# Queries and keys of an attention kernel: transposed out of the token-wise product instead of projected a second time

## The reference, cut to what matters

```
x = layernorm(tokens)                        # 8 batches, 256 tokens, 128 features
q = split(x @ Wq); k, v = split(x @ Wkv)     # 16 heads, 16 features (q, k), 64 features (v)
q, k, v = q/|q|, k/|k|, v/|v|
attn = relu(q @ k.T) ** 2                    # 256 x 256 per head
out = attn @ v
out = tanh(|out|) * out / |out|
x = tokens + out @ Wout
```

## Time and profile before

| | |
|---|---|
| time, median of 3 runs | 561.87 us (561.01 to 563.82) |
| the profiled execution: its own time, its span | 564.94 us, 563.0 us |
| mean granted clock of TensorE | 0.985 |
| attention | about the first 229 us |
| busy: PE, DVE, ACT, POOL | 530.1, 425.2, 376.3, 327.3 us |

### The profile page before, as it was taken

The page is one execution under the profiler, slowest core; times in us unless marked ns, Lnnn a source line. Parts: engine busy times, 40 slices in busy tenths (PEclk is TensorE's granted clock), DMA queues, the critical chain, the costliest instruction groups (busy, mean ns, idle before and its releaser), DMA issues.

```text
span 563.0 us, 10120 instructions
## 1 busy us (share of the span) xinstructions
PE 530.1 (94%) x3280; PEld 400.5 (71%) x3280; DVE 425.2 (76%) x1006; ACT 376.3 (67%) x676; POOL 327.3 (58%) x276
## 2 busy tenths in 40 slices
PE   5788799999999998899999999999999999999997
PEld 4555467676666665586877787787787888888885
DVE  5966868787879687449849869769769768677675
ACT  6687958677779775364466776776775775755644
POOL 2743929384846564077646756646656656566563
PEclk9899989999999999699999999999999999999999
DMA  8200000000000012910085480650751751761920
GB/s 227 86 16 14 23 15 17 15 15 15 16 16 15 15 24 64 225 30 1 6 199 103 111 197 26 171 137 24 187 123 29 183 122 48 180 139 38 223 62 19
DMA packets 36099, 44.73 MB, mean 79 GB/s; under 512 B 5456, under 2 KB 18896, under 8 KB 36048
## 3 DMA queue, kind: packets, MB, share of 16 engines
q1 hardware_dynamic: 31360, 42.40, 31.7%
q10 hardware_dynamic: 4688, 1.71, 1.3%
HBM read 40.94 MB, written 3.15 MB: 78 GB/s over the span
## 4 chain that ended last, share of the span: by engine, by line
PE 69%; DVE 11%; issue 7%; ACT 7%; POOL 3%; DMA 1%; SPq 0%; ACTq 0%; DVEq 0%; POOLq 0%
PE PS L1220 66%; DVE aT L866 4%; DVE n L845 3%; POOL hl L499 2%; ACT sqv L547 2%; ACT v L540 2%; ACT rl L565 1%; DMA Osb<-wa_dram 1%; PE PS L1355 1%; DMA wbc<-w_dram 1%; PE PS L1341 1%; DVE wfl L911 0%; PE PS L1474 0%; PE PS L1313 0%; ACT n2T L581 0%
## 5 line engine op out<-in xcount | busy, mean ns | idle before, releaser
L499 POOL TENSOR_TENSOR hl<-hb,hh 128x512 fp32r<-128x512 f32 x127 | 164.3, 1294 | 133.7 <-ACT hh L709 129.5
L702 ACT ACTIVATE sil<-PS 128x512 f32<-128x512 f32 (+1 forms) x136 | 80.8, 594 | 82.8 <-PE PS L1220 82.0
L1087 DVE TENSOR_TENSOR PS<-sil,PS 128x512 f32<-128x512 f32 x128 | 88.3, 690 | 61.0 <-PE PS L1220 39.1
L1220 PE MATMUL PS<-fxh,wfh 128*128 128x512 f32 x264 | 105.2, 398 | 3.1 <-issue 1.7
L1220 PE MATMUL PS<-fxl,wfh 128*128 128x512 f32 x264 | 105.0, 398 | 0.0
L1220 PE MATMUL PS<-fxh,wfl 128*128 128x512 f32 x264 | 104.7, 397 | 0.0
L709 ACT ACTIVATE hh<-hb 128x512 fp32r<-128x512 f32 x128 | 80.3, 627 | 32.5 <-DVE hb L1092 30.7
L1092 DVE TENSOR_TENSOR hb<-PS,wbc 128x512 f32<-128x512 f32 x128 | 88.5, 691 | 9.3 <-issue 3.2
L866 DVE SCALAR_TENSOR_TENSOR aT<-PS,rl 128x1024 f32<-128x1024 f32 x64 | 75.2, 1217 | 7.7 <-ACT rl L565 7.6
L565 ACT ACTIVATE rl<-PS 128x1024 f32<-128x1024 f32 x64 | 62.1, 1026 | 21.9 <-PE PS L1220 21.8
L424 POOL TENSOR_TENSOR sr<-n2o,half 128x32 f32<-128x32 f32 x7 | 38.2, 5462 | 51.5 <-DVE n2o L873 51.5
(11 more groups left out here) (175 smaller groups left out, 902.7 us busy)
## 6 DMA issues: line engine op xcount, KB each, us to landing
wbc<-w_dram SPq DMA_DIRECT2D x48, 512.0 KB, 11.6
wbc<-w_dram SPq DMA_DIRECT2D x32, 128.0 KB, 2.9
wbc<-w_dram SPq DMA_DIRECT2D x16, 256.0 KB, 4.2
wfs<-wf_dram SPq DMA_DIRECT2D x32, 98.0 KB, 2.0
band_dram<-zero SPq DMA_DIRECT2D x16, 80.0 KB, 1.7
band<-band_dram ACTq DMA_DIRECT2D x4, 320.0 KB, 3.1
X<-x_dram SPq DMA_DIRECT2D x1, 896.0 KB, 7.7
Osb<-wa_dram SPq DMA_DIRECT2D x3, 256.0 KB, 3.7
```

Of the source, the lines that this page charges most:

```text
L499: g.tensor_tensor(hl[:, n % RING, :], hb[:, n % RING, :], hh[:, n % RING, :].bitcast(F32), ALU.subtract).then_inc(F("hl"), 1)
L702: s.activation(sil[0:rows, n % 2, :], PS[0:rows, G0 + n % 2, :], ACT.Silu).then_inc(F("silu"), 1)
L1087: v_.tensor_tensor(PS[:, bank, :], sil[:, n % 2, :], PS[:, bank, :], ALU.mult).then_inc(F("t"), 1)
L1220: return nc.tensor.matmul(o, w, m, start=start, stop=stop)
```

## The change

The second projection goes. ACT copies the token-wise product of q and k to SBUF, into a buffer `qkt` in which the query heads lie 32 columns apart with zeros between, and PE transposes 128 columns of it at a time into the bank where the padded projection used to go. POOL squares the copy; DVE sums the squares, later in its order than before. A memset on POOL at the start zeroes the query part of `qkt` (576 columns in each of two tiles). The 768 padded weight columns are neither loaded nor split. For the first batch ACT squares the bank itself, after the copies. The diff, cut to its core:

```diff
-FIRST_WEIGHTS = (..., ("in_wp", slice(W_QK, W_V)),
-                 ("in_wq", slice(0, W_QK)))
+FIRST_WEIGHTS = (..., ("in_wp", slice(W_QK, W_V)))
+            qkt = ab("qkt", [P, 2, QT])
 @@ POOL, start
             g.memset(gr[:, :, TOPG:], -9.0).then_inc(cs("sel1"), 1)
+            g.memset(qkt[:, :, 0:NG * QG], 0.0).then_inc(cs("qkz"), 1)
             g.memset(Fpad[:, :, :], 0.0).then_inc(cs("fpad"), 1)
             g.memset(ind[:, :, :], 0.0).then_inc(cs("ind0"), 1)
             inverse_deviation(0)
+            def square_pairs(n, t):
+                pool.wait_ge(A("qkc"), 2 * n + t + 1)
+                pool.wait_ge(A("n2q"), 2 * (n - 1) + t + 1)
+                g.tensor_tensor(by_head(sqqk[:, t, 0:QK]), q_heads(t), q_heads(t), ALU.mult).then_inc(A("sqq"), 1)
+                pool.wait_ge(*freed("qk", n, t))
+                g.tensor_tensor(sqqk[:, t, QK:2 * QK], k_heads(t), k_heads(t), ALU.mult).then_inc(A("sqq"), 1)
 @@ POOL, loop
                     inverse_deviation(b + 2)
+                if b + 1 < B:
+                    square_pairs(b + 1, 0)
+                    square_pairs(b + 1, 1)
                 if b:
                     output_norms(b - 1)
 @@ ACT
-            def square_pairs(n, t):
+            def keep_pairs(n, t):
                 act.wait_ge(*full("qk", n, t))
+                if n:
+                    act.wait_ge(*full("g", n - 1, NQ - 1))
+                    after(act, A("sqq"), 4 * (n - 2) + 2 * t + 2)
+                bank = bank_of("qk", n, t)
+                s.activation(q_heads(t), by_head(PS[:, bank, 0:QK]), ACT.Copy).then_inc(A("qkc"), 1)
+                signal = free_of("qk", n, t) if n else A("qkk0")
+                s.activation(k_heads(t), PS[:, bank, QK:2 * QK], ACT.Copy).then_inc(signal, 1)
+            def first_square_pairs(t):
+                s.activation(sqqk[:, t, :], PS[:, bank_of("qk", 0, t), :], ACT.Square).then_inc(free_of("qk", 0, t), 1)
 @@ ACT, start
-            first_weights_high(3)
...
-            square_pairs(0, 0)
-            square_pairs(0, 1)
+            act.wait_ge(cs("qkz"), 1)
+            for t in range(2):
+                keep_pairs(0, t)
+            for t in range(2):
+                first_square_pairs(t)
             square_values(0, 1)
 @@ ACT, loop
                 relu(NG * b + 1)
                 if more:
-                    square_pairs(n, 0)
-                    square_pairs(n, 1)
+                    keep_pairs(n, 0)
+                    keep_pairs(n, 1)
 @@ DVE, loop
                 squares(NG * b + 1)
-                if more:
-                    pair_norms(n, 0)
-                    pair_norms(n, 1)
...
                 squares(NG * b + 2)
                 if more:
+                    pair_norms(n, 0)
+                    pair_norms(n, 1)
                     value_norms(n, 0)
                     clear_norms(n, 0)
 @@ PE
             def group(n, j):
+                for t in range(2):
+                    if j != 1:
+                        pe.wait_ge(A("qkc"), 2 * n + t + 1)
+                    elif n:
+                        pe.wait_ge(*freed("qk", n, t))
+                    else:
+                        pe.wait_ge(A("qkk0"), t + 1)
                 bank, done = turn("g", n, j)
                 for part in range(2):
-                    cols = slice((2 * j + part) * P, (2 * j + part + 1) * P)
-                    last = split3(PS[:, bank, part * L:(part + 1) * L], wah[:, cols], wal[:, cols],
-                                  xTh[:, :], xTl[:, :])
+                    cols = k_cols(part) if j == 1 else q_cols(j + part)
+                    for t in range(2):
+                        last = nc.tensor.transpose(PS[:, bank, part * L + t * P:part * L + (t + 1) * P], qkt[:, t, cols],
+                                                   ident[:, :])
```

More of the change, by code:

```diff
@@ L40 @@
 NQ = NG // 2 + 1
-WQ_G, WK_G = (0, 1, 4, 5), (2, 3)
-W_QK = 2 * NQ * P
-W_V = W_QK + 2 * QK
+W_QK, W_V = 0, 2 * QK
+QG = P + DK
+QT = NG * QG + 2 * P
 WA = W_V + H * DV
-FIRST_WEIGHTS = (("in_wv0", slice(W_V, W_V + 512)), ("in_wv1", slice(W_V + 512, WA)), ("in_wp", slice(W_QK, W_V)),
-                 ("in_wq", slice(0, W_QK)))
+FIRST_WEIGHTS = (("in_wv0", slice(W_V, W_V + 512)), ("in_wv1", slice(W_V + 512, WA)), ("in_wp", slice(W_QK, W_V)))
 WG0, WU0, WD0, WS0 = 0, NE * P, 2 * NE * P, 3 * NE * P
@@ L204, in hybrid_layer @@
         Z = Sems(ctx, nc, "full0 full5 full6 full7 free0 free5 free6 free7")
-        ld = Sems(ctx, nc, "in_x0 in_x in_wv0 in_wv1 in_wq in_wp in_wo in_wf0 in_wf1 in_sd in_gw in_wb in_bb zeroed")
-        cs = Sems(ctx, nc, "id0 id half rid ind0 ind rm rf sel fpad zero sel1 sdz wah wal wfh wfl sdh sdl")
-        A = Sems(ctx, nc, "stats mv ve rstd xn xTh vraw sqv n2v n2q nm nm_v rr vi vc0 vc vp S relu a av Oc sqO "
+        ld = Sems(ctx, nc, "in_x0 in_x in_wv0 in_wv1 in_wp in_wo in_wf0 in_wf1 in_sd in_gw in_wb in_bb zeroed")
+        cs = Sems(ctx, nc, "id0 id half rid ind0 ind rm rf sel fpad zero sel1 sdz wah wal wfh wfl sdh sdl qkz")
+        A = Sems(ctx, nc, "stats mv ve rstd xn xTh vraw sqv n2v n2q nm nm_v rr vi vc0 vc vp qkc qkk0 sqq S relu a av Oc sqO "
                           "sr sr_half n th nmx rec f1 ff fhi f")
@@ L301, in hybrid_layer, with q_cols, k_cols, q_heads @@
         fxh, fxl, wbc = (fxh0, fxh1), (fxl0, fxl1), (wbc0, wbc1)
+        def q_cols(g):
+            return slice(QG * g - DK * (g % 2), QG * g - DK * (g % 2) + P)
+        def k_cols(f):
+            return slice(NG * QG + f * P, NG * QG + (f + 1) * P)
+        def q_heads(t):
+            slots = qkt[:, t, 0:NG * QG].rearrange("p (g x) -> p g x", x=QG)[:, :, 0:P]
+            return slots.rearrange("p g (r y) -> p g r y", y=SLOT)[:, :, :, 0:DK]
+        def k_heads(t):
+            return qkt[:, t, NG * QG:QT]
+        def by_head(x):
+            return x.rearrange("p (g r d) -> p g r d", g=NG, r=HG)
+        def k_by_group(x):
+            return x.rearrange("p (f r a) -> p f a r", f=2, r=HG)
+        def heads_by_group(x):
+            return x.rearrange("p (f a r) -> p f a r", f=2, a=2)
         block = ctx.enter_context(nc.Block())
@@ L467, in _ @@
             pool.wait_ge(A("vi"), 2)
-            g.tensor_tensor(vc[:, 1, :], vi[:, 1, :], rr[:, 0, 1, H:2 * H], ALU.mult).then_inc(A("vc"), 2)
+            g.tensor_tensor(heads_by_group(vc[:, 1, :]), heads_by_group(vi[:, 1, :]), k_by_group(rr[:, 0, 1, H:2 * H]), ALU.mult).then_inc(A("vc"), 2)
             scale_values(0, 1)
@@ L848, in pair_norms @@
             def pair_norms(n, t):
-                dve.wait_ge(*freed("qk", n, t))
+                if n:
+                    dve.wait_ge(A("sqq"), 4 * (n - 1) + 2 * t + 2)
+                else:
+                    dve.wait_ge(*freed("qk", 0, t))
                 v_.tensor_reduce(n2[:, n % 3, t, 0:2 * H], sqqk[:, t, :].rearrange("p (h d) -> p h d", d=DK),
@@ L1008, in _ @@
             first_weights_low(2)
-            first_weights_low(3)
             value_norms(0, 0)
@@ L1266, in score @@
                 b, g = divmod(i, NG)
-                jq, q0, k0 = WQ_G[g] // 2, WQ_G[g] % 2 * L, g // 2 * L
+                jq, q0, k0 = g // 2 * 2, g % 2 * L, g // 2 * L
                 pe.wait_ge(*freed("g", b, jq))
@@ L1367, in _ @@
             pairs(0, 1)
-            pe.wait_ge(cs("wal"), 4)
             group(0, 0)
@@ L1591, in layout @@
     wk, wv = wkv[:, :, :DK], wkv[:, :, DK:]
[L1592 to L1597, removed]
+    wa = np.concatenate([wq, wk.reshape(D, 2, 2, HG, DK).transpose(0, 1, 3, 2, 4).reshape(D, H * DK), wv.reshape(D, H * DV)], axis=1)
     eg = np.asarray(L0_ffn_expert_gate).transpose(2, 0, 1).reshape(D, E * I)
```

7 lines of the change are left out of this document (3 added, 4 removed).

## The result

| | before | after |
|---|---|---|
| time, median | 562.56 us (561.01 to 563.82, 4 runs) | 572.09 us (570.26 to 575.36, 4 runs) |
| ratio | | 1.019, 95% interval 1.0156 to 1.0223 |
| profiled execution: its time, span, mean clock | 564.94, 563.0 us, 0.985 | 570.26, 568.5 us, 0.979 |
| start of the last squares of the attention | 220.67 us | 228.25 us |

The forecast was 571.6 us. The two medians alone divide to 1.017. The profiled execution is the fastest of the four of the changed kernel, and that of before lies above its median, so the two traces differ by less (5.5 us in span) than the medians (9.5). The last row of the table is the cleaner measure: it leaves out the expert stage, whose length differs between the profiled executions of all kernels here by almost 5 us (337.6 to 342.3), much of it with the clock at its beginning. The attention became 7.6 us longer.

What follows compares the result with a forecast made beforehand. The ACT and DVE exchange was taken to bound the stretch before score(4b+4), PE the rest of each batch. DVE 4.6, start 1.9 and clock 3.2 sum to 9.7 us on 561.87: 571.6 us, range 564.5 to 579.

Steps and rivals of the forecast that it cites:

- What binds: Before score(4b+4), the exchange between ACT and DVE sets the pace, not PE; from that score on PE does.
- DVE: In the loop, pair sums moved ahead of the values' sums add 0.65 us in seven batches: 4.6 us (3.3 to 5.6).
- ACT and POOL in the loop: ACT's four copies and POOL's four products per batch fit into existing waits: 0 us.
- Start: Before score(0), POOL's memset adds 0.86 us and ACT's copies and squares ahead of the kept groups 1.0: 1.9 us together.
- PE: Transposes replacing matmuls save 0.6 us a batch ahead of score(4b+4), where PE waits for DVE: counted as 0.
- Clock: Longer PE waits before score(4b+4) bring two more falls of TensorE's clock: 3.2 us (0 to 10).
- two or more stretches beyond those of before: Sign in the new profile: the granted clock shows at least two additional half-clock stretches.
- rival 2: TensorE's clock falls in nearly every batch, transposes not keeping it up like matmuls: 578 us, chance 0.2.
- Rival 3: Moved sums on DVE are hidden, leaving only the start and at most one clock fall: 563 to 565 us, chance 0.13.
- rival 4: PE binds, so its saved 5 us count in full: faster, 559 us, chance 0.06.

Runs made afterwards that it cites:

- the move alone: Kernel before with only the pair sums (`pair_norms`) moved behind squares(4b+2) on DVE, whole projection kept: 567.0 us, ratio 1.0091.
- the run of the start: Changed kernel with the `qkt` memset moved behind the first deviation and batch 0's groups kept before squaring the second tile's values: 570.3 us, ratio 1.0134.

## Why the prediction was right

1. **What binds.** Right. Each batch has a stretch that the exchange of ACT and DVE bounds, and PE's busy share hid it. Filling PE's wait made nothing slower, emptying it made nothing faster, and two buffers for the exchange made the kernel faster; the table of one batch shows it free of the clock.
2. **DVE.** 0.65 us a batch predicted, 0.61 to 0.62 measured, in seven batches; the move alone costs 5.1 us of median (3.4 us of the traced attention) and undoing it gives back 4.1 us of the attention. The last batch that has it gets 0.3 back at its end, where PE was not waiting. 4.0 us in all, 4.6 predicted.
3. **ACT and POOL in the loop.** Nothing, as predicted: copies 0.26 apart with 1.06 of waiting behind, products of 0.61 to 0.62 us each, 3.46 ahead of the next work.
4. **Start.** 1.9 us predicted. Score(0) is 2.0 later and the first squares 2.1. The parts fit too (memset 1.06 for 1.05, 0.88 of it on the path for 0.86), with one thing missed: beside the memsets DVE's four comparisons (L860) took 1.53 us instead of 0.67, which the wait for `ind0` covered.
5. **PE.** 0.6 us a batch saved and worth nothing, as taken. The gap before score(4b+4) is 1.64 where 1.8 was said, and a middle batch takes 27.2 us as said.
6. **Clock.** Two more falls, 3.2 us, were predicted. The trace has one stretch more, in batch 0, and a longer one at the start, which the prediction did not count; the sign "two or more stretches beyond those of before" did not come. The attention lost 5.1 us more to the clock (8.5 against 3.4), of which 7.6 - 2.1 - 4.0 = 1.5 us reached its end; in the middle batches both kernels ran at full clock. So the traced term is half of the predicted one. The 9.5 us of the medians are 1.9 us more than the 7.6 of the attention, and no trace shows where: the mean clocks of two of the three slower executions of the changed kernel (0.978 and 0.979) are those of the profiled one (0.979), though their spans are 1.3 and 2.3 us longer; only the slowest has a lower one (0.972, a span 5.1 us longer). That the sum hit the median within a microsecond is in part luck, for this reason. The sign of the term is shown: less work on PE lowered the mean clock, and work put into its wait raised it above that of every execution of the changed kernel. The rule of the Trainium skill ("TensorE: Matmul & The Clock Gate", Part 4: PE-mode transpose) that transposes do not keep the clock up like matmuls would have made rival 2 the outcome. The runs speak against it: doubling the transposes raised the clock as matmuls in their place did, with 1.7 us lost in the traced attention against 5.1, and ratios of 1.0144 and 1.0138.

Rival 3 (hidden sums) fell by the two runs that moved them, rival 4 (PE binds) by the filled and the emptied wait, rival 2 by the middle batches at full clock in the trace and by the slowest execution, 575.36 us, which is below its 578. Why the medians differ by 9.5 us and the attentions by 7.6, and why the sums' return gave 8.5 and 4.1, stays open beyond the clock at the beginning of the expert stage in the profiled executions.

## What to carry to other kernels

Work taken off an engine counts only up to the next engine's readiness at the wait where they meet; so before moving work off an engine that is busy 97% of a stretch, find the wait that releases it and see who ends it. An operation moved past one slack wait into another's chain costs its full length less the idle time found there, and that is two rows of a timeline. Where TensorE waits anyway, less work for it can cost time through its clock, and a small operation on DVE can be dear beside a POOL instruction on SBUF (1.85 us for 0.3), so look at what POOL does where you put it.

## What the runs showed of the hardware that I had not expected

**DVE held up by POOL.** DVE instructions took longer beside a POOL instruction on SBUF, in some cases until just behind its end: `weight_low`, a difference of two SBUF tensors, 1.85 us for 0.3 beside the scaling of the values; the normalisation, a one-input operation from SBUF to SBUF, 1.13 for 0.60 beside a memset; the four comparisons 1.53 for 0.67 beside the memsets at the start of the changed kernel, and 0.67 again where the long memset is moved away (the run of the start). The kernel before has it too: the floor of the output norms (its L878), 0.28 us in the changed kernel's batch 3, takes 0.90 us at 119.30 beside the scaling of the values and ends 0.05 us behind it. The squares, which read PSUM and SBUF, and the sums took the same everywhere (1217 ns a square in both kernels' pages). Nor did the one-input floor of the norms (L902, 0.19 us at 119.69) suffer from the power on POOL that ran from 114.59 to 120.05, nor `weight_low`, with its two SBUF tensors, from the next one (changed kernel, batch 3):

```profile
122.61 0.30 DVE L957 TENSOR_TENSOR wfl<-wfs,wfh 128x196 fp32r<-128x196 f32 x1
```

```profile
120.34 2.90 POOL L441 TENSOR_TENSOR vi<-nm,half 128x16 f32<-128x16 f32 x1
```

The Trainium skill, "GPSIMD Engine Reference", Specifications, says that POOL shares its SBUF interfaces with DVE and contends with 2-port modes and two-SBUF-input instructions; the trace agrees for `weight_low`, and adds that the price is up to the rest of POOL's instruction and that a POOL power did not ask it. For the instructions with one SBUF tensor no row shows whether they ran in such a mode.

**TensorE's clock and removed work.** Twelve matmuls less in each batch cost 5.5 us (567.38 against 561.92). After a wait of 1.85 us in a batch where it had been 0.57, the clock was at 1.2 GHz; in the changed kernel's batch 3 a wait of 1.64 us left it at 2.4. And one kernel's executions differ by it: in the 28 of the kernel before that ran beside the first experiments the span is 557.3 to 563.5 us at mean clocks of 0.997 to 0.982.
